# Maxima over partitions on TensorE and VectorE, and a rearranged prologue, in a kernel of gated cross-attention and a routed FFN

## The reference

```python
def _ws(w): return (w - mean(w)) * rsqrt(var(w) + 1e-5)      # row by row
def _conv(x, w, b, mask): return (einsum('oc,bct->bot', _ws(w), x) + b) * mask

n1 = layernorm(x)                                            # over 1024
q, k, v = _conv(y, wq, bq, mask_cond), _conv(y, wk, bk, mask_cond), _conv(n1, wv, bv, mask)
scores = softmax(q_head @ k_head.T / SCALE)                  # 8 heads of 32 x 32
a = _conv(scores @ v_head, wo, bo, mask) + n1
x = x + tanh(g_xattn) * (norm over channels(a) * gamma + beta) * mask

xr = layernorm(x).reshape(4096, 1024)
gates, idx = normalized top 2 of softmax(xr @ wr.T)          # 8 columns
h = silu(silu(xr @ w1.T) @ w3.T) @ w2.T
out = zeros; out[idx[:, k]] += gates[:, k] * h               # idx < 8
x = x + tanh(g_ffn) * out
```

## Time and profile before

| what | value |
| --- | --- |
| median of 3 runs | 1189.77 us (1189.12 to 1190.26) |
| the profiled execution | 1190.6 us, of which the span of the trace is 1188.8 us |
| mean granted clock of PE | 0.982 of full speed |
| PE busy | 1081.3 us, 91% of the span |
| DVE, ACT, POOL busy | 811.4, 471.3, 403.0 us |

### The profile page before, as it was taken

One profiled execution on the slowest core, in us unless ns is written; L12 is line 12 of the kernel. 1 busy time (PEld: TensorE's weight loads), 2 busy tenths in 40 slices (PEclk: granted clock), 3 DMA queues, 4 the chain that ended last, 5 costly groups with the idle time before them and its releaser, 6 DMA issues.

```text
span 1188.8 us, 18482 instructions
## 1 busy us (share of the span) xinstructions
PE 1081.3 (91%) x6871; PEld 634.0 (53%) x6871; DVE 811.4 (68%) x1951; ACT 471.3 (40%) x762; POOL 403.0 (34%) x500
## 2 busy tenths in 40 slices
PE   0646599999999999999999999999999999999998
PEld 0335456655556555654556555654556555654452
DVE  4589667985688657974788657974798558963321
ACT  3662534244234524353234524253235524252331
POOL 2193112650168013740167013740267014730000
PEclk9988699999999999999999999999999999999999
DMA  9802300040002400050002300140003300013000
GB/s 282 196 0 71 142 1 1 19 162 34 1 1 63 151 2 1 25 188 2 1 1 89 125 2 1 44 169 2 1 1 108 106 2 1 1 71 144 1 1 2
DMA packets 35215, 65.79 MB, mean 55 GB/s; under 512 B 1758, under 2 KB 19748, under 8 KB 35132
## 3 DMA queue, kind: packets, MB, share of 16 engines
q1 hardware_dynamic: 33660, 63.25, 16.1%
q10 hardware_dynamic: 1472, 1.31, 0.4%
HBM read 47.75 MB, written 16.81 MB: 54 GB/s over the span
## 4 chain that ended last, share of the span: by engine, by line
PE 57%; DVE 22%; POOL 8%; issue 6%; ACT 5%; DMA 1%; ACTq 0%; POOLq 0%; DVEq 0%
PE bank L616 39%; PE bank L487 6%; DVE ub L1075 6%; DVE ub L1094 3%; DVE ub L1090 2%; POOL xbuf L384 2%; PE bank L568 2%; PE bank L496 2%; POOL mtmp L381 2%; POOL coc L340 2%; DVE bst L1030 2%; DVE act_t L1188 1%; DVE bst L1085 1%; ACT ub L794 1%; PE bank L554 1%
## 5 line engine op out<-in xcount | busy, mean ns | idle before, releaser
L616 PE MATMUL bank<-xt_hi,w1b 128*128 128x512 f16 x1024 | 326.8, 381 | 11.1 <-DVE act_t L1188 7.1
L616 PE MATMUL bank<-w3b,h_hi 128*128 128x512 f16 x1024 | 305.0, 379 | 0.0
L616 PE MATMUL bank<-xt_lo,w1b 128*128 128x512 f16 x512 | 195.0, 381 | 0.0
L616 PE MATMUL bank<-w3b,h_lo 128*128 128x512 f16 x512 | 194.2, 379 | 0.0
L817 ACT ACTIVATE act_t<-bank,fs 128x512 f32<-128x512 f32 x128 | 87.3, 682 | 219.6 <-PE bank L616 219.6
L616 PEld LDWEIGHTS bank<-xt_hi,w1b 128*128 128x128 f16 x1024 | 100.5, 98 | 126.0 <-DVE act_t L1188 7.6
L1188 DVE SCALAR_TENSOR_TENSOR act_t<-act_t,bank 128x512 f32<-128x512 f32 x128 | 86.2, 673 | 117.9 <-ACT act_t L817 117.2
L1193 DVE SCALAR_TENSOR_TENSOR h_lo<-act_t,h_hi 128x512 f16<-128x512 f32 x128 | 98.3, 768 | 91.5 <-ACT h_hi L823 91.5
L823 ACT ACTIVATE h_hi<-act_t 128x512 f16<-128x512 f32 x128 | 80.6, 630 | 183.2 <-DVE act_t L1188 183.2
L400 POOL TENSOR_TENSOR ub<-bo_b,mcur 128x512 f32<-128x512 f32 x64 | 65.0, 1045 | 213.3 <-DVE dg L1052 213.3
L616 PEld LDWEIGHTS bank<-w3b,h_hi 128*128 128x128 f16 x1024 | 99.3, 98 | 66.8
(11 more groups left out here) (189 smaller groups left out, 1882.8 us busy)
## 6 DMA issues: line engine op xcount, KB each, us to landing
xbuf<-in_x_dram SPq DMA_DIRECT2D x16, 1024.0 KB, 5.8
out_dram<-xbuf SPq DMA_DIRECT2D x16, 1024.0 KB, 5.3
x_lo<-in_ctx_dram SPq DMA_DIRECT2D x16, 512.0 KB, 3.5
mrow<-in_mask_dram SPq DMA_DIRECT2D x16, 512.0 KB, 4.4
w1b<-in_w_dram SPq DMA_DIRECT2D x8, 512.0 KB, 7.3
w3b<-in_w_dram SPq DMA_DIRECT2D x8, 512.0 KB, 7.3
xbuf<-in_w_dram SPq DMA_DIRECT2D x1, 4096.0 KB, 14.2
ub<-in_wq_dram ACTq DMA_DIRECT2D x1, 256.0 KB
```

What stands on the lines that cost most here:

```text
L616: mm = pe.matmul(bk[:, :], left, right, start=d == 0 and n == 0, stop=d == FT - 1 and n == 2)
```

## The change

The maxima over the partitions leave POOL. PE transposes the column of 128 maxima to a row (`y_columns`, `w_columns`), DVE takes the maximum of the row and copies it along 128 columns (`y_row`, `w_row`), and PE multiplies it with a corner of the unit matrix, which puts it on all partitions (`y_spread`, `w_spread`). `y_scale` reads it from PSUM. For the pairs to come PE does `y_columns` at step 1 of stage 12 and `y_spread` at step 1 of stage 13. There are six such pairs in the FFN's part of the program (one in the written-out first pair, five in the loop), and one in the prologue.

```diff
-W1_TR = range(3, 7)
+W1_TR = (4, 5, 6, 9)
...
@@ POOL
-            def y_largest(j, n):
-                pool.wait_ge(sm["y_max"], 2 * j + 2)
-                pool.tensor_tensor(pspare[:, :], minus[:, 0:1], minus[:, 0:1], ALU.mult)
-                pool.partition_all_reduce(ms[:, 1, 0:n], ms[:, 0, 0:n], P, RMAX).then_inc(sm["y_all"], 1)
...
-                if s in (1, 2) and first_pair(j):
-                    add_beta(j, s - 1, 0)
-                    add_beta(j, s - 1, 1)
+                if s == 6 and first_pair(j):
+                    for b in range(2):
+                        add_beta(j, b, 0)
+                        add_beta(j, b, 1)
...
+            coefs(0, mvc, coc, 8, EPS, 1.0, "ws", None)
             ln1(0)
             ln1(1)
-            coefs(0, mvc, coc, 8, EPS, 1.0, "ws", None)
-            pool.wait_ge(sm["w_max"], 1)
-            y_largest(0, 4)
@@ PE
+            def y_columns(j):
+                pe.wait_ge(sm["y_max"], 2 * j + 2)
+                if first_pair(j - 1):
+                    pe.wait_ge(sm["w_lo"], 16)
+                pe.transpose(rbk[0:2, P:2 * P], ms[:, 0, 0:2], ident[:, :]).then_inc(sm["y_col"], 1)
+            def y_spread(j):
+                pe.wait_ge(sm["y_row"], j + 1)
+                pe.matmul(rbk[:, 2 * P:2 * P + 2], yrow, ident[0:2, 0:2], start=True, stop=True).then_inc(sm["y_all"], 1)
...
-            def attention(j, s, d):
+            def attention(j, s, d, jn=None):
                 b = s % 2
+                if d == 1 and jn is not None and s in (12, 13):
+                    (y_columns, y_spread)[s - 12](jn)
...
             for s in range(STAGES):
+                for d in range(FT):
+                    attention(0, s, d, 1)
+                if s in (0, 3, 10):
+                    w_columns((0, 3, 10).index(s))
+                if s in (1, 4, 11):
+                    w_spread((1, 4, 11).index(s))
                 if s in W1_TR:
                     for i in range(4):
-                        weight(4 * (s - W1_TR[0]) + i)
-                for d in range(FT):
-                    attention(0, s, d)
+                        weight(4 * W1_TR.index(s) + i)
...
-            with pe.Fori(0, PAIRS - 2) as i:
+            with pe.Fori(0, PAIRS - 3) as i:
                 for g in range(1, GROUPS + 1):
-                    group(i + 1, g, i + 2)
+                    group(i + 1, g, i + 2, jn=i + 3)
@@ ACT
-            for b in range(2):
-                normed(b, b, co, sm["ln1_coef"], sm["xs_ready"])
...
-            row_sums(0)
             for s in range(STAGES):
+                attention(0, s)
+                attention_late(0, s, 1)
+                if s == 1:
+                    small_high()
+                if s in (0, 1):
+                    normed(s, s, co, sm["ln1_coef"], sm["xs_ready"])
+                if s in (2, 4):
+                    b = (s - 2) // 2
+                    act.wait_ge(sm["qk_mm"], CT * (b + 1))
+                    act.activation(x_hi[:, b], xs[b], ACT.Copy).then_inc(sm["xhi_ready"], 1)
+                if s == 0:
+                    row_sums(0, range(0, 2))
+                if s == 1:
+                    row_sums(0, range(2, 5))
+                if s == 2:
+                    row_sums(0, range(5, FT))
@@ DVE
+            def y_row(j):
+                dve.wait_ge(sm["y_col"], j + 1)
+                dve.tensor_reduce(ms[0:2, 1, 0:1], rbk[0:2, P:2 * P], AX.X, ALU.max).then_inc(sm["y_top"], 1)
+                dve.wait_ge(sm["y_top"], j + 1)
+                dve.tensor_copy(yrow, ms[0:2, 1, 0:1].broadcast_to([2, P])).then_inc(sm["y_row"], 1)
...
                 if s in (10, 11):
                     y_largest(j, s - 10)
+                if s == 12:
+                    y_row(j)
                 if s == 13:
                     y_scale(j)
...
             for s in range(STAGES):
...
                 attention(0, s)
                 y_next(1, s)
                 if s == 0:
+                    w_row(0)
+                    ln1(0, 0)
+                if s == 1:
+                    small_low()
+                    ln1(0, 1)
+                if s == 2:
+                    row_largest(0)
+                if s == 3:
+                    w_row(1)
+                if s == 4:
                     weight_scale(0)
```

More of the change, by code:

```diff
@@ L54 @@
 MS = 8.0
[L55 to L56 removed]
+SMALL = 16 * 11
+W1_TR = (4, 5, 6, 9)
 ROUTER_FIRST = (7, 8, 9)
@@ L1281, in last_sums @@
                     .then_inc(sm["acs_set"], 1)
-            ln1(0, 0)
-            ln1(0, 1)
-            prepare()
+            weights_ready()
+            for b in range(2):
+                y_largest(0, b)
+            y_row(0)
+            y_scale(0)
+            qk_low()
             for b in range(2):
                 y_low(0, b)
+            mask_tables()
             masks(0)
+            biases()
             for s in range(STAGES):
-                if s in W1_TR:
-                    for i in range(4):
-                        weight(4 * (s - W1_TR[0]) + i)
                 attention(0, s)
```

175 lines of the change are left out of this document (98 added, 77 removed).

## The result

The changed kernel takes 1267.66 us (median of 4 runs, 1266.06 to 1271.02) where the kernel before took 1190.01 in the runs beside it: a ratio of 1.0652 with an interval of 1.0622 to 1.0681. It is slower, 8.7 us above the 1259 of the prediction and inside its range.

A forecast was written before the change was run, and what follows sets the result against it. PE was taken as the bound from the first FFN product on, a chain over all engines before it. 1190.6 + 41 (waits) + 15 (clock) + 13 (head) = 1259.6, less 0.8: 1259 us, range 1238 to 1272.

The forecast's parts named there:

- three marks: Signs against it: idle before transposes under 2 us, rows behind them at full clock, first FFN product before 147.
- two waits in six pairs: PE waits for DVE's maximum (4.5 us) and copied row (2.3 us) in groups 13 and 14: 41 us, 38 to 44.
- low clock behind them: PE's granted clock falls behind each wait: 2.55 us per pair, 15 us in six pairs, 10 to 20.
- POOL freed in the pairs, with the new chain in its place: In the six pairs, freeing POOL of the all-reduce gains nothing, as its reader `y_scale` has 5.2 us of slack.
- head: Stretch up to the first FFN product: gains 9.5 us at first projection, then loses it; +13 us, bounds -5 to +18.
- The 1.7 behind the first wait: Work PE loses to the low clock in the 4 us behind the first wait of a pair: 1.7 us.
- Rival 4: POOL's idle ahead of the all-reduce was the bound in the pairs; removal returns 5.86 us each, 1224 us; chance 0.06.
- rival 3: Not slower: DVE gets to the maxima early, PE passes both waits; 1185 or about 1190 us; chance 0.04.
- the lateness stays at about 4: In the head, behind item 1's scores (3.5 us late), DVE carries the delay through item 1's softmax at about 4 us.
- the 2 for w1's scale: In the head, w1's scale and first transposes come behind the second product with wv: about 2 us more lateness.
- 4 to 5.6 more: In the head, both items' bias tiles on DVE run beside POOL's `x_low` and moved `add_beta`: 4 to 5.6 us longer.
- 2 back: End of the head: y's and w3's maxima lose the all-reduce's idle but add trips over PE and DVE; 2 us regained.

The follow-up runs named there:

- experiment 1: Changed kernel with both the transpose of y's maxima and the spreading product moved from step 1 to step 7 of stages 12 and 13: 1206.75 us.
- Experiments 1 to 3: Changed kernel with step 7 in place of step 1 for both instructions (1206.75 us), only the spreading product (1247.64), only the transpose (1230.21).
- the last of experiments 4 to 7: experiment 1 with 136 products that nobody reads put into PE's idle times in the head: 1206.68 us.
- experiment 9: Changed kernel with both instructions late and the head rearranged (1181.36 us), then the first pair's maximum of y given back to POOL's all-reduce: 1185.79 us.

## Why the prediction was right, and where it was off

The sign, the mechanism and the range were right, by the steps that were given, and none of the three marks came that would have shown it wrong (an idle under 2 us, the full level behind the transposes, a first FFN product before 147). Its marks for the later head were off: the long product came at 104.89, not near 99, and the first FFN product at 161.87, not near 155. The sizes, of the 80.4 us between the two spans:

| term | predicted | measured | from |
| --- | --- | --- | --- |
| two waits in six pairs | 41 (38 to 44) | 38.5 | the idle before L427 and L432 |
| low clock behind them | 15 (10 to 20) | 20.9 | below |
| POOL freed in the pairs, with the new chain in its place | 0 | 0.9 lost | experiment 1 against before, from the first FFN product on |
| head | 13 (-5 to 18) | 19.9 | first FFN product, 161.87 - 142.00 |

These sum to 80.2.

**The waits.** 4.5 and 2.3 per pair were predicted from the two chains on DVE, with the new product itself in each; 4.16 and 2.06 were measured as idle alone, 5.30 in the first pair. The second maximum still stands behind an eviction on DVE, as in the earlier trace rows. Experiments 1 to 3 show that it is these waits and that they add.

**The clock.** From the first FFN product to the end the changed kernel takes 1107.3 (1269.2 - 161.87) and the one with both waits filled 1080.9 (1243.0 - 162.10). Of the 26.4 between them 5.5 are the idle before w1's products, which is about as long in experiment 1 (5.8) and in the kernel before (7.1 besides the 3.9 ahead of the first of them) and therefore no part of the change's price. This leaves 20.9. Two other ways come to the same: 59.7 less the 38.5 of idle is 21.2 (experiment 1), and the stretches behind the two waits are 14.2 and 6.4 longer than with both filled, together 20.6. Of the 20.9, 16.4 stand in the two rows of w3's products alone (316.1 + 199.6 against 305.0 + 194.3). The 1.7 behind the first wait was too low: 14.2 in six pairs is 2.4 each. Behind the second the 1.7 was near for each fall (6.4 in four is 1.6), but the clock fell in four of six pairs, and the prediction had counted it by half. The prediction weighed this against the under 1% that the Trainium skill (TensorE: Matmul & The Clock Gate, Part 1, The HAM clock gate) gives for a clock coming up; measured are 20.9 of 1269.2, or 1.6%, so the trace goes against that figure here.

**POOL's part.** That its all-reduce had 5.2 us of slack in the pairs holds: with the waits out of the way nothing is gained on balance by its removal (1047.7 against 1046.8). Rival 4, with 5.86 back in each of six pairs, would have put that some 35 lower, so it falls, and rival 3 with the idle rows.

**The head** is the term that was mis-sized: +13 in the prediction, +19.9 in this profile. Six other runs with the same instructions in the head have the first FFN product between 157.93 and 162.45, so the term is 16 to 20.5. Its early marks were near: first projection 30.5 against 30.95, exponential 48 against the row of ACT here:

```profile
48.91 0.24 ACT L787 ACTIVATE dg<-dg 128x64 f32<-128x64 f32 x1
```

The step that failed is "the lateness stays at about 4", with the 2 for w1's scale behind it: by the bias tiles the head was 10.1 late, not 6. 1.9 of the missing 4.1 came with the scores (63.92 for 62); with the rest goes PE at the lower of its levels (1.2 of 2.4 GHz), with a mean granted clock of 0.59 between 60 and 80 us: scores that take 3.60 for 1.95, transposes of w1 that take 3.5 for 1.9. The prediction charged the clock in the pairs alone. The unread products in the head (the last of experiments 4 to 7) bring the scores to the full clock and the bias tiles 3.3 forward, but the median did not gain; 1.1 of the 3.3 went to the collision of DVE with POOL, and for the rest there is no reason to show. That collision was in the prediction (4 to 5.6 more) and cost 4.2 in the rows; taking it away brought 9.2. A second term was left out: the lot of w1's blocks that now stands behind item 1's bias tiles (2.7), so that `attention_out` was 17 late and not 11. The blocks between the residuals cost 2.7 for the 3.7 assumed. And "2 back" at the end did not come: from the end of the last statistics to the first FFN product it is 13.8 us against 13.6.

## What to carry to other kernels

An engine that is the bound must not meet a wait in the middle of its stream: here the same two instructions six steps later cost about 1 us in place of 60. Price such a wait as its idle plus what the clock takes behind it (here half as much again), and look for the place in the program where the producer is done. When small work is moved out of idle time, ask what it meets at its new place: normalisation ahead of a softmax and POOL's additions beside DVE's tiles cost the head 14 us, more than the 9 that it had won.

## What the runs showed of the hardware that was not expected

Filling idle time on PE with unread products paid little here unless it was done at both places: 3.4 and 4.5 us for one each, 25.2 for both. With the first alone filled the low clock came behind the second wait in all six pairs, where it had come in four. An idle of 1.1 to 1.8 before a product of w1, in the four pairs in the middle, went with it: 5.8 us in experiment 1, 12.4 with the first wait filled (where it comes twice in a pair), none with both. It is older than the change: PE's loop made six passes before (of PE's program only the last pair was written out behind it) and makes five now, and this idle stood at five places before (7.1 us) and stands at four now, one less than the passes each time. The trace names for it "issue", or a VectorE row that ends at about that time; in some pairs PE starts before that row has ended, so it isn't the cause. What sets this idle was not tried and stays open.

The all-reduce over partitions costs POOL far more than the 0.37 us of its row: in experiment 9 POOL does nothing for 7.41 us ahead of it and 8.11 behind it, and but for 3.4 of the second the profile shows nothing that it waits for. In the kernel before, all eight rows of L356 have such an idle ahead of them, 49.8 us together. Right ahead of such an idle stand two instructions MODIFY_POOL_CONFIG on POOL's queue (at 20.5 and 20.6 in experiment 9); whether they are the cause was not tried. The chain that replaces the all-reduce takes 0.27 + 0.21 us of DVE and three small products of PE.
